# Weights stage of a graph kernel: one transfer for the coefficients, node rows loaded later, four store buffers, reload split 7 to 1

## The reference

```python
xn = _layernorm(x, axis=-1)
# in each of the two graph layers l:
W = jnp.einsum('rb,bio->rio', coeffs[l], bases[l])    # (8,30) x (30,256,256)
h = jnp.einsum('ni,rio->rno', x, W)                   # a table of 8 rows per node
msg = h[edge_type, src] * deg_inv[dst][:, None]
x_new = segment_sum(msg, dst) + x @ self_loops[l]
# then a linear attention over the nodes, and a routed feed-forward with 32 experts
```

## Time and profile before

| | us |
|---|---|
| median of 3 executions | 2637.95 |
| lowest, highest | 2635.55, 2640.66 |
| the profiled execution | 2638.15 |
| its span, first to last instruction | 2635.7 |
| TensorE busy | 2187.0 (83%) |
| VectorE, ScalarE busy | 927.4, 665.2 |
| GpSimd busy | 1639.7 (62%) |
| mean granted TensorE clock | 0.932 |

### The profile page before, as it was taken

One profiled execution on the slowest core, in us unless ns is written; L12 is line 12 of the kernel. 1 busy time (PEld: TensorE's weight loads), 2 busy tenths in 40 slices (PEclk: granted clock), 3 DMA queues, 4 the chain that ended last, 5 costly groups with the idle time before them and its releaser, 6 DMA issues. The chain is left out here.

```text
span 2635.7 us, 37803 instructions
## 1 busy us (share of the span) xinstructions
PE 2187.0 (83%) x9589; PEld 1617.7 (61%) x9592; DVE 927.4 (35%) x2885; ACT 665.2 (25%) x1463; POOL 1639.7 (62%) x1713
## 2 busy tenths in 40 slices
PE   5899986999999989998996877777777777775398
PEld 1478874676676666766765656656665566554165
DVE  1320003333333333333332444444434444445154
ACT  3455541121122111211212122222222222200055
POOL 0000007777777777777773777777777777774756
PEclk9999998999999999999997988998899889988699
DMA  9964446555555555555553443434344344333443
GB/s 222 278 193 179 191 180 174 169 175 177 170 168 173 187 173 168 173 181 168 168 168 121 119 116 117 120 116 116 116 118 118 116 117 121 116 116 105 126 145 116
DMA packets 155583, 401.30 MB, mean 152 GB/s; under 512 B 35295, under 2 KB 86850, under 8 KB 140285
## 3 DMA queue, kind: packets, MB, share of 16 engines
q0 software_dynamic: 81648, 219.65, 28.4%
q10 hardware_dynamic: 36372, 126.22, 12.9%
q1 hardware_dynamic: 37434, 53.89, 7.6%
HBM read 262.67 MB, written 141.04 MB: 153 GB/s over the span
## 5 line engine op out<-in xcount | busy, mean ns | idle before, releaser
L476 POOL DMA_INDIRECT gnn_ring<-table,g_idx x1564 | 1504.1, 962 | 723.6 <-issue 474.0
L519 PE MATMUL gnn_pagg<-gnn_ring,gnn_oh 128*128 x3904 | 1046.2, 414 | 284.9 <-PEq L48 240.2
L519 PEld LDWEIGHTS gnn_pagg<-gnn_ring,gnn_oh 128*128 128x128 f32 x3904 | 737.7, 201 | 554.6 <-issue 448.9
L503 DVE TENSOR_TENSOR gnn_oh<-gnn_col,g_dst 128x256 f32<-128x256 f32 x976 | 409.6, 426 | 1008.5 <-DVEq L48 1007.4
L749 ACT COPY gnn_rows<-gnn_pm 128x512 f32<-128x512 f32 x196 | 115.3, 588 | 763.3 <-PE gnn_pm L703 763.3
L998 ACT ACTIVATE gnn_qe<-gnn_pq,gnn_bq 128x128 f32<-128x128 f32 x98 | 36.0, 368 | 709.2 <-PE gnn_pq L976 709.2
L351 PE MATMUL pre_psum<-pre_whigh,pre_high 128*128 128x512 f32 x392 | 157.5, 402 | 10.9 <-DVE pre_low L279 10.4
L703 PE MATMUL gnn_pm<-gnn_whigh,gnn_high 128*128 128x512 f32 x392 | 158.1, 403 | 0.0
L351 PE MATMUL pre_psum<-pre_whigh,pre_low 128*128 128x512 f32 x392 | 153.8, 392 | 0.0
L703 PE MATMUL gnn_pm<-gnn_whigh,gnn_low 128*128 128x512 f32 x392 | 153.7, 392 | 0.0
L703 PE MATMUL gnn_pm<-gnn_wlow,gnn_high 128*128 128x512 f32 x392 | 153.4, 391 | 0.0
(11 more groups left out here) (172 smaller groups left out, 2317.1 us busy)
## 6 DMA issues: line engine op xcount, KB each, us to landing
table<-pre_rows ACTq DMA_DIRECT2D x49, 1024.0 KB, 3.9
table<-gnn_rows ACTq DMA_DIRECT2D x49, 1024.0 KB, 4.5
gnn_ring<-table,g_idx POOLq DMA_INDIRECT x1564, 2.8
pre_bs<-in_L_gnn_bases SPq DMA_DIRECT2D x64, 240.0 KB, 7.6
bucket<-gnn_zrow SPq DMA_DIRECT2D x16, 650.0 KB
g_xT<-bucket SPq DMA_DIRECT2D x20, 520.0 KB
x1T<-gnn_x1T ACTq DMA_DIRECT2D x49, 128.0 KB
gnn_x1T<-x1T ACTq DMA_DIRECT2D x49, 128.0 KB, 2.7
```

The source lines that it names most:

```text
L476: eng.indirect_dma_start(self.ring[:, q % RG, t, 0:D], None, self.g.table[self.l][:, :], bass.IndirectOffsetOnAxis(ap=self.g.idx[:, at:at ...
L503: self.nc.vector.tensor_tensor(self.oh[:, h, :, :], self.col[:, :].unsqueeze(1).to_broadcast([P, n, P]), self.g.dst[:, ds(q * TPG + h * n, ...
L519: mm = nc.tensor.matmul(pagg[:, k, 0:self.width], self.oh[:, h, i, :], self.ring[:, ds(q & (RG - 1), 1), t, 0:self.width].rearrange("p o n ...
```

## The change

The coefficients come as one array that the host has already laid out block-diagonally (120 rows of 256 bytes), in one DMA at the head of SP's queue. Pieces 0 to 7 follow one another on SP with no node rows between them; r0 stands behind piece 7, r1 behind the reloads. Writes of layer 0's pieces leave from 4 buffers, two of which lie in parts of `xs` whose node rows are not loaded yet. The reload is split 7 pieces to 1: 56 partitions x 8 x 1 KB in each of the first 4 DMAs, 8 partitions x 8 x 1 KB in each of the last 4. On VectorE only chunk 0 is normalised ahead of `wlow`, and the other chunks stand one place later by the same rhythm; `root(0)` stands behind all of layer 0's pieces on ScalarE, and `edges()` two blocks later.

```diff
+    WB = 4
-        w_out = [s.sem(f"w_out{k}") for k in range(2)]
+        w_out = [s.sem(f"w_out{k}") for k in range(WB)]
+        def stage(n):
+            if n % WB < 2 or n >= NPC:
+                return wst[:, n % 2, :]
+            at = 4 * G + (n % WB - 2) * (PIECE // D)
+            return xs[0:4 * R, at:at + PIECE // D, :].rearrange("p b d -> p (b d)")
...
+            eng.dma_start(cf[:, :, :], a["coeff_blocks"]).then_inc(cf_in, 16)
             for n in range(NPC):
                 load(n)
-                if n == BUF - 1:
-                    rows_in(0)
-                if n == BUF + 1:
-                    rows_in(1)
-            for j in range(2):
-                for k in range(2):
-                    eng.wait_ge(w_out[k], 16 * (j + 1) * NPC // 4)
-                load_weights(eng, g, rows, 0, wr_in[j], j * D // 8, (j + 1) * D // 8)
+            rows_in(0)
+            for j, (lo, hi) in enumerate(((0, NPC - 1), (NPC - 1, NPC))):
+                for k in range(WB):
+                    eng.wait_ge(w_out[k], 16 * ((hi + WB - 1 - k) // WB))
+                load_weights(eng, g, rows, 0, wr_in[j], lo * PIECE // D, hi * PIECE // D)
+            rows_in(1)
             for n in range(NPC, NPC + BUF):
                 rows_in(n - NPC + 2)
                 load(n)
...
-            eng.memset(cf[:, :, :], 0.0).then_inc(cf_zero, 1)
...
-            for c in range(2):
-                stats(c)
-                norm(c)
+            stats(0)
+            norm(0)
...
-                if c + 2 < NCH:
-                    norm(c + 2) if late else stats(c + 2)
-                elif c + 2 == NCH and not late:
+                if c + 1 < NCH:
+                    norm(c + 1) if late else stats(c + 1)
+                elif c + 1 == NCH and not late:
                     edges()
...
-            eng.wait_ge(cf_in, 128)
+            eng.wait_ge(cf_in, 16)
...
             def weights(n):
-                if n >= 2:
-                    eng.wait_ge(w_out[n % 2], 16 * (n // 2))
+                l, c = divmod(n, NPC)
+                k, earlier = (c % 2, NPC // WB + c // 2) if l else (c % WB, c // WB)
+                if earlier:
+                    eng.wait_ge(w_out[k], 16 * earlier)
...
-            eng.wait_ge(cf_zero, 1)
-            for l in range(2):
-                for q in range(4):
-                    eng.dma_start(cf[q * NBASE:(q + 1) * NBASE, l, q * R:(q + 1) * R], a["L0_gnn_coeffs"][l]).then_inc(cf_in, 16)
             for n in range(NPC):
                 weights(n)
-                if n == NPC // 2:
-                    root(0)
-            root(1)
+            root(0)
...
-                if b % 2 == 0 and b // 2 + 2 < NCH:
-                    root(b // 2 + 2)
+                if b % 2 == 0 and b // 2 + 1 < NCH:
+                    root(b // 2 + 1)
```

More of the change, by code:

```diff
@@ L172, in startup @@
         bi_ok, bi_out, bound_in = (s.sem(n) for n in ("bi_ok", "bi_out", "bound_in"))
-        cf_zero, cf_in, w_ps, w_sb = (s.sem(n) for n in ("cf_zero", "cf_in", "w_ps", "w_sb"))
+        cf_in, w_ps, w_sb = (s.sem(n) for n in ("cf_in", "w_ps", "w_sb"))
         wr_in = [s.sem(f"wr_in{k}") for k in range(2)]
         bs_in = [s.sem(f"bs_in{k}") for k in range(BUF)]
-        w_out = [s.sem(f"w_out{k}") for k in range(2)]
+        w_out = [s.sem(f"w_out{k}") for k in range(WB)]
         whigh_ok, wlow_ok, high_ok, low_ok, chunk_ok, chunk_free = (s.sem(n) for n in (
@@ L386, in weights @@
                     eng.wait_ge(w_ps, i + 1)
-                    nc.scalar.copy(wst[:, n % 2, q * 512:(q + 1) * 512], psum[0:4 * R, 6 + i % 2, :]).then_inc(w_sb, 1)
+                    nc.scalar.copy(stage(n)[:, q * 512:(q + 1) * 512], psum[0:4 * R, 6 + i % 2, :]).then_inc(w_sb, 1)
                 eng.wait_ge(w_sb, 4 * n + 4)
-                l, c = divmod(n, NPC)
-                eng.dma_start(g.wrel[l * 4 * R:(l + 1) * 4 * R, c * PIECE:(c + 1) * PIECE], wst[:, n % 2, :]).then_inc(w_out[n % 2], 16)
+                eng.dma_start(g.wrel[l * 4 * R:(l + 1) * 4 * R, c * PIECE:(c + 1) * PIECE], stage(n)).then_inc(w_out[k], 16)
             def high_part(b):
@@ L433, in _ @@
                 eng.wait_ge(stored[k], 16 * ((NB + 1 - k) // 2))
-                eng.wait_ge(w_out[k], 16 * NW // 2)
+            for k in range(WB):
+                eng.wait_ge(w_out[k], 16 * (NPC // WB + (NPC // 2 if k < 2 else 0)))
 class Aggregate:
@@ L1261 @@
     layout["edge_type_8"] = by_partition(np.asarray(inputs["edge_type_8"]), 0)
-    layout["L0_gnn_coeffs"] = np.asarray(inputs["L0_gnn_coeffs"]).transpose(0, 2, 1)
+    coeffs = np.asarray(layout.pop("L0_gnn_coeffs"))
+    blocks = np.zeros((4, NBASE, 2, 4, R), np.float32)
+    for q in range(4):
+        blocks[q, :, :, q, :] = coeffs.transpose(2, 0, 1)
+    layout["coeff_blocks"] = blocks.reshape(4 * NBASE, 2, 4 * R)
     layout["L0_mix_bq"] = np.asarray(inputs["L0_mix_bq"]).reshape(H2, P).T
```

## The result

The changed kernel is slower: 2647.06 us (median of 8 executions, 2640.35 to 2649.95) against 2637.04 (8 executions, 2628.86 to 2640.89), a ratio of 1.0031 with a 95% interval of 1.0022 to 1.0041. The forecast was 2635.8 with a range up to 2641.5. The profiled execution has 2649.95 us, the longest of the eight, and a span of 2648.1, 12.4 more than the span before.

What follows compares the result with a forecast made beforehand. The prediction took TensorE to be bound through its last wait, p11, behind a full DMA queue; only p11's 2.2 us gain counted, the other parts hiding: 2637.95 - 2.2 = 2635.8 us, range 2630.5 to 2641.5.

Steps and rivals of the forecast that it cites:

- What bounds the kernel: TensorE is busy from 120 us on; a lead at the first multiply counts only as far as p11 lands earlier.
- Part 5: Queue behind the reload: same transfers plus r1 stand before p11, bytes conserved; p11 at 107.0, 2.2 us earlier.
- Part 1: Start of the weights: coefficients in one DMA let TensorE start at about 8.35 instead of 13.58, p3 issued at 14.8.
- Part 2: Pieces 3 to 7: no gaps and 4.92 us per piece, so p7 lands at 42.8, 7.6 us earlier.
- Part 4: Node chunk 0: r0 lands at 46.1, its work ends at 57.7, hidden under `whigh` at 59.3.
- Part 3: Write and reload: large reload takes 10.2 us, small one 1.2, so `whigh` starts at 59.3, 5.6 earlier.
- rival A: Small reload takes 4.7 us instead of 1.2, what follows is 3.5 later: +1.3, 2639.3 us; chance 0.25.
- Part 6: Clock in PE's gap at p11: same low-clock cost as before, p11's matmuls taking 6.37 instead of 3.70 us.
- Part 7: Moved VectorE work: chunk 1's normalising hides with 5 us of slack, later `edges()` costs 0.
- D: Large reload of 56 partitions takes twice 10.2 us, p11 lands 10.2 later: +8.0, 2646 us; chance 0.08.
- C: Coefficients come no sooner: TensorE starts at 13.6, the queue's dry 2.5 us returns: 2638.3 us; chance 0.05.
- B: p11 is not bound by the queue, the full 5.6 us lead reaches the end: 2632.3 us; chance 0.15.

Runs made afterwards that it cites:

- e9_rows_spread_2: e1_halves with SP's queue behind the reload reordered, one chunk of node rows after each base piece; 2620.71 us against 2639.31, ratio 0.993.
- e10_order_alone: Kernel before, with only SP's queue behind the reload reordered to alternate base pieces and node rows; 2629.87 us against 2639.31, ratio 0.9965.
- e7_coeffs_alone: Kernel before, with only the coefficients in one transfer at the head of SP's queue; on a slower chip 3725.24 us, ratio 1.0034 (0.9987 to 1.008).
- e1_halves: Changed kernel with its reload split 4 pieces to 4 again, 32 partitions per DMA; 2633.68 us against 2638.94 for the kernel before, ratio 0.998.
- e3_six_two: Changed kernel with its reload split 6 pieces to 2, 48 and 16 partitions per DMA; 2639.36 us, ratio 1.0002 to the kernel before.
- e4_r1_early: Changed kernel with r1 moved in front of the reload, behind r0, 7 to 1 split kept; 2645.14 us, ratio 1.0023 to the kernel before.
- e6_skewed_r1: e1_halves with r1 brought by two DMAs of 119 and 9 partitions; on a slower chip 3727.55 us, ratio 1.0055 to the kernel before.

## Why the prediction was wrong

- **What bounds the kernel** held. A lead at the first multiply counts only as far as p11 lands earlier, and what p11 loses reaches the end: 12.6 us at p11, 12.8 at the table's end, 12.4 in the span. In the other kernels whose last wait is p11 the shifts there and at the table's end agree within 1.7 us. e9_rows_spread_2 and e10_order_alone, where TensorE waits for no piece, gain about the 2.7 us of p11's low clock besides (11.4 at p11 and 14.5 at the table's end in the former). The bound itself was a matter of order, as e10_order_alone and e9_rows_spread_2 show, and not of bytes as part 5's conservation put it: the node rows in front of p11 could wait.
- **Part 1** held: TensorE at 8.44 (forecast 8.35), p3's wait gone. In e7_coeffs_alone it brings little by itself: p11 is 0.3 us later than before and the table's end 1.4 earlier.
- **Part 2** held as a price, though this execution missed it by 1.4 us: p7 at 44.21, not 42.8, with 5.2 us between pieces and not 4.92. The other kernels with the same instructions up to there have p7 at 41.9 to 43.0, e1_halves at 42.51. That the reload was issued at 47.89 as forecast is luck: p6's write left 1.3 us late (43.56, not 42.25) and took 4.2 us instead of 5.5. **Part 4** held: r0's `stats` began at 47.18 (forecast 46.1), and it was no bound.
- **Part 3 failed**, in its step "the rate of the same transfer kind". The large reload took 12.7 us from issue to end, not 10.2, the small one 3.8, not 1.2: about 5.2 us in all, with whigh at 64.45 and not 59.3. A DMA of 56 partitions took 2.7 us where I had scaled 1.18 us by bytes to 2.07, and one of 8 took 1.0 where I had 0.3. I had counted the ports that a transfer reaches, and held it against the small reload only, as rival A, which priced it at 4.7 against the 3.8 measured. The table above fits the fullest port instead. "The 56-partition DMAs keep my 2.07 us" was the wrong reading: by the Trainium skill's map ("SBUF — State Buffer", on the DMA port swizzle) 56 partitions put 8 on six of their eight ports, where 32 put 4 on each.
- **Part 5 failed**, in the step from "stood 44.4 us behind the reload's end" to "the same transfers stand before it and r1 besides": whigh to p11 took 57.3 us, not 47.7. 2.4 of the 9.6 too many are there without a lag too (50.1 in e1_halves, 49.5 in e3_six_two); 7.2 come with it, as a difference of single executions. That engines which finish late hold up everything queued behind was no term of the sum and no rival. Rival A's "if the DMA engines do not catch up" came near and priced it at 3.5; it is 5.2 before whigh and 7.2 behind it.
- **Part 6** was about right: p11's matmuls took 6.31 us, with the clock at 0.60 of full over the wait. **Part 7** held: behind the first multiply TensorE waits for base pieces and, for 0.8 us, for ScalarE, and never for node rows.
- Of the **rivals**, D had the sign and the right transfer, but its price (twice the time of the large reload) and its mechanism were not what happened. C is out with TensorE's start at 8.44. B was refuted by e1_halves for this order.

Left open: how much of the 7.2 us at p11 comes from the 14 engines of the large reload and how much from the 8 of the small one. The increments of e4_r1_early have groups for both, 4.7 and 3.1 us apart, but no run has one without the other.

## What to carry to other kernels

Before you resize a transfer, count its partitions twice: for the fullest port, which fits the time of each transfer here, and for the number of engines that will share it, which sets how far they fall behind the rest; keep the count a multiple of 16. In a full queue the order is the lever: bring what the busiest engine needs next, then the rest, one piece at a time. A lead that is won at the front must be followed to the last wait before the busiest engine runs without one.

## What the runs showed of the hardware

- A lag between DMA engines survives in a full queue: in e6_skewed_r1 at least 6.2 us lie between the groups of 9 and 7 engines at r2 and 5.5 at r3, some 10 us later. From 60 to 110 us the queue moves 233 to 253 GB/s in the four kernels with such a lag and 278 to 310 in the others, at a busy share of 1.02 to 1.06 and 0.99 to 1.04, so the DMA share doesn't show it; GB/s and the spread of a transfer's increments do.
- The base pieces' DMAs, 30 partitions each, get 15 increments as their data lands, in every kernel, and one engine runs ahead: before the change r5 gets its first increment at 83.1 and the other fifteen at 95.5 to 97.2. No run tried another cut of the bases.
- DMAs of 8, 16 and 32 partitions with 8 KB in each take about the same time, 1.0 to 1.2 us; one of 48 takes 2.5.
- One chip ran what follows the table's end 1070 to 1100 us slower (2637 against 3723 us in all) while the first stage kept its times: whigh at 58.2 there and at 58.5 on the other chip, for the same kernel.
